# An attention block on one core: a third home buffer, the first group's diagonal squares copied by GpSimd, and 11 pairs of key tiles parted into heads and tails

## The reference

```
y      = group_norm(x, 4 groups) * gamma + beta          x: 4 x 128 x 32 x 32, fp32; N = 1024 positions
q,k,v  = w_qkv y + b_qkv
scores = q^T k * 128^-0.5                                1024 x 1024 for each of 4 batches
w      = softmax(scores)
out    = x + w_out (w v) + b_out
```

## Time and profile before

| | us |
|---|---|
| median of 3 runs | 137.77 (137.07 to 138.37) |
| the profiled execution | 138.07 |
| its span, first to last instruction | 136.3 |
| TensorE busy | 129.4 |
| VectorE busy | 99.8 |
| ScalarE busy | 65.0 |
| GpSimd busy | 41.4 |

### The profile page before, as it was taken

The page is one execution under the profiler, slowest core; times in us unless marked ns, Lnnn a source line. Parts: engine busy times, 40 slices in busy tenths (PEclk is TensorE's granted clock), DMA queues, the critical chain, the costliest instruction groups (busy, mean ns, idle before and its releaser), DMA issues.

```text
span 136.3 us, 1759 instructions
## 1 busy us (share of the span) xinstructions
PE 129.4 (95%) x543; PEld 89.1 (65%) x543; DVE 99.8 (73%) x170; ACT 65.0 (48%) x117; POOL 41.4 (30%) x49
## 2 busy tenths in 40 slices
PE   6999999998999949999999999999999999999990
PEld 6987688875777526666666666666656577554670
DVE  0589699999998996877686889866868886761302
ACT  3154778854675372544542475544633474730000
POOL 6032130730022229300190058000770367303210
PEclk9999999999999999999999999999999999999999
DMA  4940000030056978985689656888888459961011
GB/s 152 350 191 0 0 5 0 3 77 0 0 111 147 210 188 236 207 203 169 154 204 206 204 114 160 191 195 224 203 202 201 122 123 209 209 176 77 0 77 77
DMA packets 8937, 19.01 MB, mean 139 GB/s; under 512 B 3040, under 2 KB 3040, under 8 KB 8928
## 3 DMA queue, kind: packets, MB, share of 16 engines
q1 hardware_dynamic: 8640, 18.63, 53.8%
q10 hardware_dynamic: 288, 0.27, 0.6%
HBM read 4.20 MB, written 2.11 MB: 46 GB/s over the span
## 4 chain that ended last, share of the span: by engine, by line
PE 75%; DVE 12%; SPq 7%; issue 2%; DMA 2%; DVEq 0%
PE mixed L833 31%; PE scores L778 7%; SPq L255 7%; PE scores L779 7%; PE scores L781 7%; DVE scores L577 5%; PE scores L839 4%; PE turned L798 3%; DVE flipped_odd L605 3%; PE turned L723 3%; DMA home_odd<-flipped_odd 2%; PE mixed L830 1%; PE mixed L828 1%; PE mixed L829 1%; PE mixed L723 1%
## 5 line engine op out<-in xcount | busy, mean ns | idle before, releaser
L577 DVE TENSOR_SCALAR_CACHE_REDUCE scores<-scores,key_bias 128x1024 f32<-128x1024 f32 x31 | 40.0, 1289 | 15.0 <-PE scores L781 14.7
L426 ACT ACTIVATE probs<-scores,neg_max 128x1024 f32<-128x1024 f32 x32 | 35.7, 1116 | 22.7 <-DVE scores L577 21.9
L833 PE MATMUL mixed<-home_odd,v 128*128 128x512 f32 x48 | 22.6, 594 | 1.9 <-DMA home_odd<-flipped_odd 1.9
L833 PE MATMUL mixed<-home_even,v 128*128 128x512 f32 x48 | 22.1, 594 | 0.0
L778 PE MATMUL scores<-y_hi_odd,z_hi_odd 128*128 128x512 f32 x32 | 18.7, 585 | 0.6 <-DVE z_lo_odd L544 0.6
L778 PE MATMUL scores<-y_hi_even,z_hi_even 128*128 128x512 f32 x30 | 15.9, 531 | 0.0
L605 DVE STREAM_TRANSPOSE flipped_odd<-probs 128x1024 f32<-128x1024 f32 x12 | 14.8, 1235 | 0.3 <-DMA home_odd<-flipped_odd 0.3
L605 DVE STREAM_TRANSPOSE flipped_even<-probs 128x1024 f32<-128x1024 f32 x12 | 14.8, 1234 | 0.0
L833 PEld LDWEIGHTS mixed<-home_even,v 128*128 128x128 f32 x48 | 8.9, 189 | 7.8 <-issue 7.2
L833 PEld LDWEIGHTS mixed<-home_odd,v 128*128 128x128 f32 x48 | 8.5, 190 | 8.3 <-issue 8.0
L779 PE MATMUL scores<-y_lo_odd,z_hi_odd 128*128 128x512 f32 x32 | 12.6, 392 | 0.0
(11 more groups left out here) (162 smaller groups left out, 202.9 us busy)
## 6 DMA issues: line engine op xcount, KB each, us to landing
home_odd<-flipped_odd SPq DMA_DIRECT2D x48, 128.0 KB, 2.4
home_even<-flipped_even SPq DMA_DIRECT2D x48, 128.0 KB, 2.4
out_dram<-result SPq DMA_DIRECT2D x8, 256.0 KB, 3.5
inv_wide<-inverse_rows SPq DMA_DIRECT2D x7, 256.0 KB, 3.6
xs<-in_x_dram SPq DMA_DIRECT2D x2, 512.0 KB, 6.5
xs<-in_x_dram SPq DMA_DIRECT2D x3, 256.0 KB, 4.6
xs<-in_x_dram ACTq DMA_DIRECT2D x1, 256.0 KB, 3.3
ws<-in_weights_dram SPq DMA_DIRECT2D x1, 256.0 KB, 4.0
```

What stands on the lines that cost most here:

```text
L426: act.activation(probs[:, i % RING, :], scores[:, i % 2, :], ACT.Exp, bias=neg_max[:, i:i + 1], scale=-1.0, accum_out=row_sum[:, i:i + 1]) ...
L577: dve.tensor_scalar(scores[:, i % 2, :], scores[:, i % 2, :], key_bias[:, b % 2, i:i + 1], None, ALU.subtract, ALU.min, accum_out=neg_max[ ...
L833: mm = pe.matmul(bank, v[:, b % 2, k, :], there, start=first, stop=final)
```

## The change

Four things change. (1) There are three homes, `home[group % 3]`; a swap waits for the mixing of the group three back. (2) Of the first swapped group (group 1) 12 pieces are sent by DMA, and the four with t = g are copied by GpSimd (`diagonal`) in slots 7 and 8. (3) Eleven pairs of key tiles are parted: pairs 2 and 3 of groups 2 to 5 and pairs 1, 2 and 3 of group 6. ScalarE rounds a pair (4 runs of 256 columns) to `heads` (`pair_head`), GpSimd subtracts the heads in place (`pair_tail`; VectorE for the last pair), and TensorE makes v_hi x head and v_lo x head (`mix_heads`) in one slot and v_hi x tail (`mix_tails`) in the next. For this v_hi is copied and v_lo subtracted for all batches. (4) The tiles are spread anew over the slots (four slots of a group: tile 0; tiles 1, 2; tile 3 and heads of pair 2; tails of pair 2 and heads of pair 3; the tails of pair 3 stand first in the next), and GpSimd's and ScalarE's work on the inputs is moved. The diff, cut to its core:

```diff
+    Y_HEAD_SLOT = {1: 1, 10: 2, 15: 3}
...
-    SWAP = 16 * SQ * SQ
-    MIX = {4: [(0, 1)], 5: [(0, 1)], 6: [(0, 1)], 7: [(0, 1)], 8: [(0, 1)], 9: [(0, 1)], 10: [(0, 2)]}
-    for group in SWAPPED:
-        for k in range(PAIRS):
-            MIX.setdefault(4 * group + 7 + k, []).append((group, 2))
+    HOMES = 3
+    PARTED = {group: (2, 3) for group in SWAPPED}
+    PARTED[SWAPPED[0]], PARTED[LAST - 1] = (), (1, 2, 3)
+    MIX = {4: 1, 5: 1, 6: 1, 7: 1, 8: 1, 9: 1, 10: 2}
...
-            return SWAP * len([g for g in SWAPPED if g <= group and g % 2 == group % 2])
+            return sum(16 * squares_sent(g) for g in SWAPPED if g <= group and g % HOMES == group % HOMES)
...
+        def pair_at_home(group, pair):
+            return home[group % HOMES][:, :].rearrange("p (g w) -> p g w", g=SQ)[:, :, 256 * pair:256 * pair + 256]
+        def pair_of_heads(pair):
+            return heads[:, pair - 1, :].rearrange("p (g w) -> p g w", g=SQ)
+        def parted_in(n):
+            group = (n - 8) // QB
+            return (group, 2 + n % QB) if group in SWAPPED[1:] and n % QB < 2 else None
...
             def swap(group):
                 sp.wait_ge(s_flipped, QB * group)
-                if group > 2:
-                    sp.wait_ge(s_mixed, KT * (group - 1))
-                for k in range(SQ):
+                if group >= HOMES:
+                    sp.wait_ge(s_mixed, KT * (group - HOMES + 1))
+                for k in range(1 if group == SWAPPED[0] else 0, SQ):
                     for g in (0, 2, 1, 3):
                         t = g ^ k
-                        sp.dma_start(home[group % 2][32 * t:32 * t + 32, g * N:(g + 1) * N],
+                        sp.dma_start(raw_home(group)[32 * t:32 * t + 32, g * N:(g + 1) * N],
                                      flipped[group % 2][32 * g:32 * g + 32, t * N:(t + 1) * N]
-                                     ).then_inc(s_swapped[group % 2], 16)
+                                     ).then_inc(s_swapped[group % HOMES], 16)
...
+            def pair_tail(group, pair):
+                pool.wait_ge(s_head, pair_number(group, pair))
+                there = pair_at_home(group, pair)
+                pool.tensor_tensor(there, there.bitcast(fp32), pair_of_heads(pair).bitcast(fp32),
+                                   ALU.subtract).then_inc(s_parted, 1)
+            def diagonal(g):
+                pool.wait_ge(s_flipped, QB)
+                if g == 0:
+                    pool.wait_ge(s_z_lo, HALVES)
+                else:
+                    pool.wait_ge(s_diagonal, g)
+                if g == 2:
+                    pool.wait_ge(s_rstd, 3)
+                pool.tensor_scalar(home_first[32 * g:32 * g + 32, g * N:(g + 1) * N], flipped[1][32 * g:32 * g + 32, g * N:(g + 1) * N],
+                                   1.0, None, ALU.mult).then_inc(s_diagonal, 1)
...
                 if b >= 2:
-                    pool.wait_ge(s_pj, job_count(b - 1, Z0))
+                    pool.wait_ge(s_pj, job_count(b - 1 if b == 2 else b - 2, Z0 if b == 2 else V2))
...
                     n = BLOCKS * b + i
-                    if b == 0 and i == 0:
+                    if parted_in(n):
+                        pair_tail(*parted_in(n))
+                    if n == 0:
                         normalised_input(1)
-                    if b == 0 and i in (2, 3):
-                        y_tail(1, i - 2)
-                    if b == BATCHES - 1 and i == 2:
-                        value_tail()
-                    if i == 5:
-                        residual(b)
-                    if b == 1 and i == 0:
-                        rstd_of(2, 4, 3)
-                    if 0 < b < BATCHES - 1 and i == 1:
-                        normalised_input(b + 1)
-                    if 0 < b < BATCHES - 1 and i == 3:
-                        y_tail(b + 1, 0)
-                    if 0 < b < BATCHES - 1 and i == 4:
-                        y_tail(b + 1, 1)
+                    if n in (2, 3):
+                        y_tail(1, n - 2)
+                    if n == 5:
+                        residual(0)
+                    if n == 6:
+                        value_tail(0)
                     if i == 7 and b + 1 < BATCHES:
                         z_tail(b + 1)
+                    if n == 8:
+                        rstd_of(2, 4, 3)
+                    if n in (7, 8):
+                        diagonal(2 * (n - 7))
+                        diagonal(2 * (n - 7) + 1)
+                        pool.wait_ge(s_diagonal, 2 * (n - 6))
+                    if n == 9:
+                        normalised_input(2)
+                    if n in (10, 11):
+                        y_tail(2, n - 10)
+                    if n == 11:
+                        value_tail(1)
+                    if n == 14:
+                        normalised_input(3)
+                    if n == 15:
+                        y_tail(3, 0)
+                        y_tail(3, 1)
+                    if n > 11 and i == 2:
+                        value_tail(b)
+                    if n > 8 and i == 6:
+                        residual(b)
                     if n >= 12 and n % QB == 0:
                         add_residual((n - 12) // QB)
                     if n + 2 >= QB * LAST and n + 2 < BATCHES * BLOCKS:
                         normalise(n + 2)
+            for pair in (1, 2):
+                pair_tail(LAST - 1, pair)
             add_residual(LAST - 2)
             add_residual(LAST - 1)
...
                 if b >= 2:
                     act.wait_ge(s_mixed, KT * (HALVES * (b - 1) - 1) + hi)
-                copied = act.activation(v[:, b % 2, lo:hi, :], tiles, ACT.Copy)
-                if b == BATCHES - 1:
-                    copied = act.activation(v_hi[:, lo:hi, :], tiles, ACT.Copy)
-                copied.then_inc(s_v, 1)
+                    act.wait_ge(s_v_lo, b - 1)
+                act.activation(v[:, b % 2, lo:hi, :], tiles, ACT.Copy)
+                act.activation(v_hi[:, b % 2, lo:hi, :], tiles, ACT.Copy).then_inc(s_v, 1)
...
+            def pair_head(group, pair):
+                act.wait_ge(s_swapped[group % HOMES], swaps(group))
+                if group == SWAPPED[0]:
+                    act.wait_ge(s_diagonal, SQ)
+                act.wait_ge(s_mixed, KT * (group - 1) + 2 * (pair + 1) if group > 1 else KT)
+                act.activation(pair_of_heads(pair), pair_at_home(group, pair).bitcast(fp32), ACT.Copy).then_inc(s_head, 1)
...
                 last = b + 1 == BATCHES
                 for i in range(BLOCKS):
+                    if last and i == BLOCKS - 1:
+                        pair_head(LAST - 1, 1)
+                        pair_head(LAST - 1, 2)
                     if not swapped(BLOCKS * b + i):
                         turned_copy(BLOCKS * b + i)
+                    if last and i == BLOCKS - 1:
+                        pair_head(LAST - 1, 3)
                     if i == 0 and b > 0:
                         projection_copy(b, V2, mixed[:, 1, :])
                     if b == 0 and i in (0, 1):
                         first_values((V1, V2)[i], mixed[:, i, :])
                     if i in JOB_SLOT and not last:
                         projection_copy(b + 1, JOB_SLOT[i], turned[:, JOB_BANK[JOB_SLOT[i]], :])
+                    if parted_in(BLOCKS * b + i):
+                        pair_head(*parted_in(BLOCKS * b + i))
                     if after(b, i, 2)[0] < BATCHES:
                         exponentials(*after(b, i, 2))
-                    if i == (1 if b == 0 else 2) and not last:
-                        y_head(b + 1)
+                    if BLOCKS * b + i in Y_HEAD_SLOT:
+                        y_head(Y_HEAD_SLOT[BLOCKS * b + i])
...
                 dve.wait_ge(s_exp, n + 1)
+                if group == 3:
+                    dve.wait_ge(s_diagonal, SQ)
                 if group > 2:
...
+            def last_pair_tail():
+                dve.wait_ge(s_head, pair_number(LAST - 1, 3))
+                there = pair_at_home(LAST - 1, 3)
+                dve.tensor_tensor(there, there.bitcast(fp32), pair_of_heads(3).bitcast(fp32),
+                                  ALU.subtract).then_inc(s_last_parted, 1)
...
+            def mix_whole(group, tiles):
+                b, g = group // HALVES, group % HALVES
+                for k in tiles:
+                    if k == 0:
+                        mix_waits(group)
+                    pe.matmul(mixed[:, g, :], v[:, b % 2, k, :], raw_tile(group, k), start=k == 0,
+                              stop=k == KT - 1).then_inc(s_mixed, 1)
+            def mix_heads(group, pair):
+                b, g = group // HALVES, group % HALVES
+                pe.wait_ge(s_v_lo, b + 1)
+                pe.wait_ge(s_head, pair_number(group, pair))
+                for k in (2 * pair, 2 * pair + 1):
+                    pe.matmul(mixed[:, g, :], v_hi[:, b % 2, k, :], tile_of_heads(k), start=False, stop=False)
```

(107 more changed lines are left out.)

57 lines of the change are left out of this document (18 added, 39 removed).

## The result

The changed kernel is slower: 142.83 us median (142.5 to 143.97, 4 runs) against 137.55 (137.07 to 138.37, 4 runs) for the kernel before, a ratio of 1.0392 (95% interval 1.0314 to 1.0471). The forecast was 135.9, at most 138.6. The profiled execution took 143.97 us, its span 142.2, against 138.07 and 136.3.

What follows compares the result with a forecast made beforehand. The prediction saw three bounding stretches: VectorE to 38 us, transfers to 51, then TensorE. Its terms summed to -2.2 us, -2.0 slot by slot, taken as -1.9 from the 137.77 us median: 135.9 us, range 134.0 to 138.6.

Steps and rivals of the forecast that it cites:

- The first swap: Group 1's swap, four transfers fewer: landing at 48.35 instead of 50.86 us, -1.85 us, with +0.35 for the y tail.
- GpSimd's four copies: Squares copied for group 1's swap: 0.28 to 1.12 us each, 1.12 taken, done by 46.8 us, before the transfers.
- rival 4: GpSimd's queue slower: pair tails longer than the value tail; 2.9 us cancels the gain, 3.3 gives 140.4 us; chance 0.15.
- TensorE's work: Mixing of 22 parted tiles: three products of 0.232 us instead of 0.86 a tile, saving 0.16 each, -3.6 us.
- rival 3: VectorE or ScalarE takes TensorE's place from slot 15; half of 3.6 us returns as waits: 137.7 us; chance 0.30.
- Z0 behind the y tail: Slot 12: Z0 needs y_tail(2, 0), ready at 51.75 us, while TensorE would be there at 51.4: +0.35 us.
- V2 of batch 3: Slot 24: V2 waits for scale(3), because a group's last tails end a slot later: +0.35 us.
- The wait for home: TensorE's wait for the first swap's landing, ending at 51.00 us, goes entirely: -1.85 us.
- Heads of the values: Batch 0: a second copy of v on ScalarE delays exp(0) and VectorE's chain up to the first swap: +0.5 us.
- The third home: Swaps with three homes: worth 0 us, since TensorE waited for the first swap alone; later swaps keep 1.6 to 3 us slack.
- The end: Slots 28 and 29: TensorE's turns 30 and 31 wait for GpSimd's normalises, +0.85 and +1.2 us.
- The last pair's tail: Group 6, on VectorE: 1.16 us, ready in time; if blocked by GpSimd, the result 0.2 us later.

Runs made afterwards that it cites:

- m1: The kernel before plus seven GpSimd copies into a buffer nobody reads, of several sizes, with one or two operations: 136.63 us, a single run.
- b1: The changed kernel with the four diagonal copies given a second operation (times 1.0 times 1.0): 137.39 us, ratio 0.9961 to the kernel before.
- c1: The kernel before with only the first swap's part (12 pieces by DMA, four two-operation GpSimd copies), two homes, nothing parted: 136.11 us, ratio 0.9893.
- a1: The changed kernel with all 16 squares of group 1 sent by DMA again, no GpSimd copies: 137.32 us, ratio 0.9938 to the kernel before.
- b7: b2 with two homes instead of three: 137.53 us, ratio 1.0019 to the kernel before.
- a3: The changed kernel with GpSimd's addition for group 5 waiting for VectorE's tail of the last pair: 143.01 us, ratio 1.0381 to the kernel before.
- b4: b1 with GpSimd's addition for group 5 waiting for VectorE's tail of the last pair: 136.67 us, ratio 0.9933 to the kernel before.
- b2: b1 with GpSimd's add_residual(4) after normalise(31) and residual(3) after the last pair tails and VectorE's: 136.10 us, ratio 0.9886 to the kernel before.

## Why the prediction was wrong

**The first swap** is the step that failed, in the term "GpSimd's four copies": "it costs between 0.28 (a quarter) and 1.12 us. I take 1.12." It is 2.77, outside both bounds (m1). The nearest row had the same element count and both of its operations; the copy has one, and the bounds were taken as if that could only save. The one row with a single operation (L294, 0.54 for 128 columns) is not in the prediction; it leaves room up to 4.3. The quarter was wrong too: partitions don't divide the time. What follows was in the prediction, as "copies of 2 us ... would slip some 3 us", but got no chance, since the bound excluded it. The price is the changed kernel against b1: 6.1 us, of which 0.66 is the start of that execution, so 5.4. Its parts: four copies take 4 x 1.73 = 6.9 us more, of which 2.06 were covered (b1's last copy ends at 47.00, its mixing starts at 49.06), and the mixing starts 5.67 later (54.73), 5.0 without the start. By scores(14) it is 6.70, another 1.0, in the stretch with the granted clock of 0.50, and that clock costs 0.3 more up to 58.2. Then b1 has its 0.92 us of waiting for the y tail, which the changed kernel is too late to need, and 6.1 is left. The time that came out was beyond the worst rival (140.4), and by the mechanism of none: GpSimd's pair tails, on which rival 4 hung, took 2.39 as forecast.

With the copy put right the step stands: the wait is gone, and the last addition of c1 comes 2.0 us earlier, 0.3 of which is its start. The transfers' side was right (12 issues in 7.6 to 7.8 us, 8.6 to 9.1 with a pause). But of the 1.85 forecast some 1.0 was a pause between two issues that comes in some executions: in m1 and a1 the 16 issues take 10.1 us and TensorE waits 0.8, not 1.9. So the profiled execution of before was dearer here than those two, and part of the 2.0 is luck of that execution.

That leaves 132.84 (b1) against the 131.0 forecast for TensorE's end, 1.8 us. The terms, forecast and as the rows give them, each wait counted from the point at which TensorE's last product before it would have let the next one start:

- **TensorE's work**, -3.6: a product costs 0.232 to 0.236 and a whole tile 0.86, so the price was right. Between scores(15) and scores(31) b1 needs 54.92 us and c1 56.29; both mix 32 tiles in it, 12 of b1's parted, and V2's wait of 0.35 lies in it, so (1.37 + 0.35) / 12 = 0.14 a tile, and 22 tiles are -3.15. By the rows alone they would be -3.4: in b1 the six products of two tiles go from 74.57 to 75.98, 0.70 a tile. The rest I can't place; it may be the handoffs, which I had put at 0.1 in all. Beyond V2's no wait for VectorE or ScalarE appeared there: rival 3 is wrong in its mechanism.
- **Z0 behind the y tail**, +0.35: in b1 TensorE could go on at 51.46 and starts at 52.54, 1.08 (its row shows 0.92), since GpSimd reaches the y tail at 51.01, not 50.47. **V2 of batch 3**, +0.35: right. TensorE could start at 94.63 and does at 94.98 (its row shows 0.19).
- **The wait for home**, -1.85: counted in the same way it was 2.0 in the kernel before, from 48.98 to 51.00, and is gone.
- **Heads of the values**, +0.5: about 0.36, within what the start varies by (c1 and b1 differ from before by -0.30 and +0.07 at scores(9)). 
- **The third home**, 0: wrong, about 1.1 us (b7), though nothing waited in the trace of before. The last tile of a group is mixed a slot later, and so a swap that has to wait for the mixing of two groups back starts later; my ledger gave it slack without working that wait out.
- **The end**, turns 30 and 31, +0.85 and +1.2: the waits came, 0.79 and 0.92 in b1; counted as above they are 0.96 and 1.09.
- **The last pair's tail**, 1.16 us, "in time": 4.28 in the changed kernel, 4.44 in b1, and TensorE stood 1.0 us for it, with what comes before and after it 1.2. VectorE's tail, which reads home and heads, ended 1.1 us after GpSimd's last instruction in a row, wherever that was moved: 131.49 and 132.57 in the changed kernel, 130.43 and 131.51 in a3, 124.14 and 125.22 in b4, 123.55 and 124.64 in b2 (2.36 in all). The Trainium skill, "SBUF — State Buffer", section "Who interferes with whom", has it that such a pair excludes one another; the traces agree, with 1.1 us of its own. The prediction cited it and gave +0.2, from 1.25 us behind pair_tail(6,2). In the changed kernel it stood 1.9 us behind that one (128.29 to 130.21) and then behind the addition, 1.3 us more: GpSimd's next instruction went ahead of VectorE's, which had been waiting.

In sum, against the forecast: tiles +0.45, Z0 +0.73, V2 0, the wait for home -0.17, the end +1.2 (0.96 + 1.09 + 1.21 = 3.3 for 2.05), the start -0.43: +1.8, where 1.8 is to be explained. With cheap copies the other parts of the change are worth nothing, because what the parted tiles save, 3.15 us, the waits for GpSimd and for the last tail take back in the last 20 us. b2 wins 1.8 of that back and ends where c1 does.

## What to carry to other kernels

A row prices another instruction only if it has the same form: operations and operands as well as elements; measure an operation that the trace does not show, or shows only over far fewer columns, above all where a bound says that it is cheap. When work is moved to an engine with idle time, write down what stands behind it in that engine's order and put your range on the case where the cover is gone. Try each part alone before taking a large change as a whole: here one line cost 5.4 us, one part alone (c1) was as fast as the best of the whole, and the others cancelled.

## What the runs showed of the hardware

- GpSimd's TENSOR_SCALAR over 1024 fp32 columns takes 2.77 us with one operation and 1.04 with two (512 columns with one: 1.49); 32, 64 and 128 partitions alike.
- VectorE's TENSOR_TENSOR with two inputs in SBUF is recorded with up to 4.44 us where 1.1 are its own, when GpSimd has instructions in a row; it ended 1.1 us after the last of them in five kernels (changed, a3, b1, b2, b4).
- TensorE's granted clock was 0.50 to 0.53 for 3.5 us after 4.8 us without a matmul, and full before and after; that cost 1.4 us.
- The issue of the first swap's 16 transfers by SyncE took 11.16 us in one execution and 10.1 in two others, by one pause of 1 us; that of 12 took 7.6 to 7.8 us in seven executions and 8.6 to 9.1 in four.
